# Layer 0's graph sum as a dense product over weights of node pairs, on one Trainium2 core

## The reference, cut to what matters

```python
edge_index = jnp.stack([src, dst])          # row = src, col = dst
def _L0_gnn_ref(x, edge_row, edge_col, edge_vals, w, b):
    deg = jax.ops.segment_sum(edge_vals, edge_row, num_segments=n)
    dinv = jnp.where(deg > 0, deg ** (-0.5), 0.0)
    norm_vals = edge_vals * dinv[edge_row] * dinv[edge_col]
    h = x @ w
    msg = norm_vals[:, None] * h[edge_col]
    agg = jax.ops.segment_sum(msg, edge_row, num_segments=n)
    return jax.nn.relu(agg + b)
x = x + _L0_gnn_ref(_layernorm(x, axis=-1), src, dst, edge_weight, L0_gnn_w, L0_gnn_b)
```

## Time and profile before

| what | value |
|---|---|
| median of 3 runs | 8010.51 us (8003.66 to 8014.09) |
| the profiled execution | 7996.99 us; span of its trace 7995.0 us |
| busy share of the span | PE 75%, PEld 54%, DVE 60%, ACT 37%, POOL 43% |
| mean granted clock of TensorE | 0.865 |
| DMA | 1231 MB, 154 GB/s over the span |

### The profile page before, as it was taken

One profiled execution on the slowest core, in us unless ns is written; L12 is line 12 of the kernel. 1 busy time (PEld: TensorE's weight loads), 2 busy tenths in 40 slices (PEclk: granted clock), 3 DMA queues, 4 the chain that ended last, 5 costly groups with the idle time before them and its releaser, 6 DMA issues. The chain is left out here.

```text
span 7995.0 us, 122318 instructions
## 1 busy us (share of the span) xinstructions
PE 5968.8 (75%) x30884; PEld 4285.4 (54%) x30885; DVE 4801.9 (60%) x10565; ACT 2966.1 (37%) x7906; POOL 3435.1 (43%) x2953
## 2 busy tenths in 40 slices
PE   7377566666663668788887696788887599587898
PEld 5155444444442435555565384566665488366666
DVE  7588533333333455788887625899998511687333
ACT  0033344444442224455554231454544333233333
POOL 1100188888884013777775041777775022000000
PEclk9855688888886779899998798999998799798999
DMA  3055699999997028777776143777776233321000
GB/s 157 31 176 177 170 190 191 189 188 186 189 191 188 4 69 318 219 230 230 231 230 162 44 135 105 231 234 239 238 236 168 101 111 103 121 99 39 8 12 20
DMA packets 671115, 1231.15 MB, mean 154 GB/s; under 512 B 93515, under 2 KB 477309, under 8 KB 658692
## 3 DMA queue, kind: packets, MB, share of 16 engines
q0 software_dynamic: 276016, 679.29, 33.9%
q1 hardware_dynamic: 388148, 540.62, 21.6%
q10 hardware_dynamic: 6560, 6.55, 0.3%
HBM read 902.62 MB, written 323.50 MB: 153 GB/s over the span
## 5 line engine op out<-in xcount | busy, mean ns | idle before, releaser
L2262 POOL DMA_INDIRECT rows<-l_kv,index_staged x1708 | 1721.4, 1008 | 706.6 <-issue 499.4
L1289 POOL DMA_INDIRECT gcn_sums<-out,target x806 | 1308.2, 1623 | 283.8 <-issue 156.8
L2375 PE MATMUL sum<-messages,hot 128*128 128x260 f32 (+1 forms) x3416 | 953.2, 408 | 53.5 <-issue 24.5
L2351 PE MATMUL q<-queries,spread 128*128 x5136 | 712.3, 285 | 129.0 <-DVE rows L2512 82.3
L2321 ACT ACTIVATE messages<-rows,messages 128x64 f32<-128x64 f32 (+1 forms) x3392 | 774.4, 323 | 0.0
L1309 PE MATMUL g<-same,hot 128*128 128x128 f32 x1612 | 319.0, 374 | 522.2 <-DVEq L1367 481.0
L2375 PEld LDWEIGHTS sum<-messages,hot 128*128 128x128 f32 x3416 | 606.4, 195 | 156.6 <-issue 74.0
L2512 DVE TENSOR_TENSOR rows<-q,rows 128x512 f32<-128x512 f32 x854 | 572.3, 683 | 142.2 <-DMA rows<-l_kv,index_staged 141.2
L2351 PEld LDWEIGHTS q<-queries,spread 128*128 128x128 bf16 x5136 | 483.3, 101 | 322.1 <-issue 218.2
L1309 PEld LDWEIGHTS g<-same,hot 128*128 128x128 f32 x1612 | 290.5, 277 | 619.4 <-issue 567.9
L1360 DVE TENSOR_SCALAR before<-before 128x13 f32<-128x13 f32 x62 | 11.3, 182 | 891.2 <-DMA gcn_sums<-out,target 890.6
(11 more groups left out here) (543 smaller groups left out, 11802.1 us busy)
## 6 DMA issues: line engine op xcount, KB each, us to landing
window<-gcn_rows SPq DMA_DIRECT2D x806, 128.0 KB
edge_counts<-count_stage SPq DMA_DIRECT2D x21, 3800.0 KB
rel<-slot_rel SPq DMA_DIRECT2D x218, 256.0 KB
src_row<-in_src_row SPq DMA_DIRECT2D x62, 832.0 KB
counts<-edge_counts SPq DMA_DIRECT2D x8, 4800.0 KB
first_part<-in_L_ffn_first SPq DMA_DIRECT2D x32, 1030.0 KB
rows<-l_kv,index_staged POOLq DMA_INDIRECT x1708
edge_attr<-in_attr SPq DMA_DIRECT2D x124, 208.0 KB
```

Of the source, the lines that this page charges most:

```text
L1289: pool.indirect_dma_start(out=copies[m], out_offset=bass.IndirectOffsetOnAxis(ap=target[:, u, j:j + 1], axis=0), in_=out[:, u, j, :], in_o ...
L2262: pool.indirect_dma_start(out=rows[:, u * 2 + n, j, :], out_offset=None, in_=table, in_offset=bass.IndirectOffsetOnAxis(ap=staged[:, u, n ...
L2351: ins = pe.matmul(q_ps[g % QUERY_BANKS][:, r, :], spread[:, t[1] * 2 + n, g * RUN % U + r, :], qs[:, bass.ds(tile, 1), m, :], start=m == 0 ...
L2375: ins = pe.matmul(sum_ps[g % 2][:, 0:W], hot[:, n, j, :], messages[:, n, j, :, :].rearrange("p h d -> p (h d)"), start=r == 0, stop=r == R ...
```

## The change

The sum of layer 0 is computed as a dense product: the weights of all edges between two nodes are added into a matrix of node pairs, and 625 float32 products (25 tiles of sources by 25 steps of 125 destinations) multiply it with the table's rows.

- The windows now take five nodes per group, so a key is one of 5 x 25 = 125 pairs; there are 97 windows in place of 108 and blocks of three windows (33, in place of 22 of five). Each window has two accumulations, each in four single-buffered PSUM banks: the counts as before (bf16) and the weights. For the weights VectorE multiplies the key one-hots with the edges' weights into float32 (`key_w`), ScalarE widens the lane one-hots to float32 (`lane_f`), and TensorE makes 15 more float32 products of 128 columns. ScalarE evicts both, and SyncE stores both for each block: counts as [128 partitions, 25, 5 x slots], weights as [125 partitions, slots, 128], with up to 46 slots in a block.
- `edge_units` also makes the weights of each unit: seven transpositions, seven ScalarE copies and 28 more products.
- `dense_sum` replaces `scatter_sum`. Its 75 steps (three groups of 10, 10 and 5 source tiles, 25 steps each) are loaded through a ring of six buffers by five DMAs of 25 partitions each; the table's rows lie in SBUF by step. The products stand between those of the edge perceptron, ten to a batch. At a group's end VectorE scales, adds bias and `x`.
- `clear_rows`, the seven copies, `CopySums`, relative positions and the count of loops fall away.

```diff
+        self.gcn_rows = nc.dram_tensor("gcn_rows", [NPAD, D], F32, kind="Internal").ap()
...
-NODES_EACH = 4
-COUNT_COLS = NODES_EACH * TILES
+NODES_EACH = 5
+PAIR_ROWS = NODES_EACH * TILES
...
-BLOCK_WINDOWS = 5
+BLOCK_WINDOWS = 3
...
+                pe.wait_ge(weight_in, 16)
+                for r, c, m in spans:
+                    real = min(m, CHUNKS - c)
+                    pe.transpose(key_ps[r // 4][0:real, r % 4 * P:(r % 4 + 1) * P], by_lane[:, c:c + real], k.ident[:, :]
+                                 ).then_inc(turned, 1)
+                pe.wait_ge(weight_rows, R)
...
+                for q, at, n in parts:
+                    pe.wait_ge(keyed, q + 1)
+                    for r, c, m in spans:
+                        ins = pe.matmul(key_ps[q][:, 0:n], weight[0:m, r, :], chosen[0:m, r, at:at + n],
+                                        start=r == 0, stop=r == R - 1)
+                ins.then_inc(weighed, 1)
...
+    k.pair_weights = nc.dram_tensor("pair_weights", [C, GROUP_SLOTS, P], F32, kind="Internal").ap()
...
+        count_stage = ph.sb("count_stage", [P, 2, TILES, BLOCK_SLOTS * E])
+        weight_stage = ph.sb("weight_stage", [P, 2, BLOCK_SLOTS * P])
+        count_ps, weight_ps = (ph.ps(n, [P, WINDOW_BANKS, 512]) for n in ("count_window", "weight_window"))
...
+                    dve.wait_ge(keys_hot, w + 1)
+                    shape = [P, U, C]
+                    dve.tensor_tensor(key_w[:, w % 2, :, :], hot_key[:, w % 2, :, :],
+                                      unit_w[:, w * U:(w + 1) * U].unsqueeze(2).to_broadcast(shape), ALU.mult
+                                      ).then_inc(keys_weighed, 1)
...
+                    begin(count_ps, P, C)
+                    if w:
+                        at = nc.snap(regs[U], min_val=0, max_val=(BLOCK_SLOTS - 1) * E)
+                        pe.matmul(counts[:, 0:C], k.ident[:, :], count_stage[:, last, :, bass.ds(at, E)].rearrange("p s e -> p e s"),
+                                  start=False, stop=False)
+                    pe.wait_ge(lanes_hot, w + 1)
+                    pe.wait_ge(keys_hot, w + 1)
                     for j in range(U):
                         at = nc.snap(regs[j], min_val=0, max_val=U * SLOT_COLS)
+                        pe.matmul(counts[:, bass.ds(at, C)], hot_lane[:, u, j, :], hot_key[:, u, j, :], start=False, stop=False)
+                    end(count_ps, P).then_inc(count_full, 1)
                     if w:
+                        pe.wait_ge(weight_kept, w)
+                    begin(weight_ps, C, P)
+                    if w:
+                        at = nc.snap(regs[U + 1], min_val=0, max_val=(BLOCK_SLOTS - 1) * P)
+                        pe.matmul(weights[0:C, 0:P], k.ident[0:C, 0:C], weight_stage[0:C, last, bass.ds(at, P)],
+                                  start=False, stop=False)
+                    pe.wait_ge(lanes_wide, w + 1)
+                    pe.wait_ge(keys_weighed, w + 1)
+                    for j in range(U):
+                        at = nc.snap(regs[j], min_val=0, max_val=U * SLOT_COLS)
+                        pe.matmul(weights[0:C, bass.ds(at, P)], key_w[:, u, j, :], lane_f[:, u, j, :], start=False, stop=False)
+                    end(weight_ps, C).then_inc(weight_full, 1)
...
+                def widen(w):
+                    act.wait_ge(lanes_hot, w + 1)
+                    act.activation(lane_f[:, w % 2, :, :], hot_lane[:, w % 2, :, :], ACT.Copy).then_inc(lanes_wide, 1)
...
+                            act.wait_ge(counts_stored, 16 * (b - 1))
+                            act.wait_ge(weights_stored, 16 * (b - 1))
...
+                    act.activation(weight_stage[0:C, b % 2, bass.ds(at, W * P)],
+                                   weight_ps[0:C, :, :].rearrange("p b c -> p (b c)"), ACT.Copy).then_inc(weight_kept, 1)
...
+                    sp.wait_ge(weight_kept, last)
+                    if b:
+                        sp.wait_ge(weights_stored, 16 * b)
+                    at = nc.snap(regs[1], min_val=0, max_val=GROUP_SLOTS - slots)
+                    sp.dma_start(k.pair_weights[:, bass.ds(at, slots), :],
+                                 weight_stage[0:C, b % 2, 0:slots * P].rearrange("p (g c) -> p g c", c=P)
+                                 ).then_inc(weights_stored, 16)
+                sp.wait_ge(counts_stored, 16 * BLOCKS)
+                sp.wait_ge(weights_stored, 16 * BLOCKS)
...
-def clear_rows(eng, tables, zeros, cleared):
...
+SUM_BANKS = 5
+SUM_TILES = 2 * SUM_BANKS
+KEYS = PAIR_ROWS // NODES_EACH
+STEP_NODES = KEYS * NODES_EACH
+STEPS_EACH = NODES // STEP_NODES
+SUM_STEPS = [(t, min(SUM_TILES, TILES - t), n) for t in range(0, TILES, SUM_TILES) for n in range(STEPS_EACH)]
+PRODUCTS = [(s, j) for s, (t, width, n) in enumerate(SUM_STEPS) for j in range(width)]
+PER_BATCH = len(PRODUCTS) // BATCHES
+SHARES = (1, 3, 5, 7, PER_BATCH)
...
+def dense_sum(k, table):
+
+    nc, a = k.nc, k.a
+    RING, S, E = 6, STEP_NODES, NODES_EACH
+    assert S * STEPS_EACH == NODES and S <= P
+    last_of = [PRODUCTS.index((s, width - 1)) // PER_BATCH for s, (t, width, n) in enumerate(SUM_STEPS)]
     with k.phase() as ph:
+        h = ph.sb("h_by_step", [P, STEPS_EACH, D])
+        pairs = ph.sb("pairs", [P, RING, SUM_TILES, P])
+        bias = ph.sb("gcn_bias", [P, D])
+        total = ph.sb("total", [P, 2, 2, D])
...
+        sum_ps = [ph.ps(f"sum{n}", [P, 2, D]) for n in range(SUM_BANKS)]
+        table_in, bias_in, pairs_in = ph.sem("table_in"), ph.sem("bias_in"), [ph.sem(f"pairs_in{n}") for n in range(RING)]
+        used, summed, emptied, scaled = (ph.sem(n) for n in ("used", "summed", "emptied", "scaled"))
+        weights = k.pair_weights.rearrange("(n t) g c -> n t g c", n=E)
+        rows = table[0:NODES, :].rearrange("(s g n) d -> n g s d", n=E, g=KEYS)
+        banks = [(t, b, min(2, width - 2 * b)) for t, width, n in SUM_STEPS if n == 0 for b in range(-(-width // 2))]
...
+                def load(s):
+                    t, width, n = SUM_STEPS[s]
+                    if s >= RING:
+                        sp.wait_ge(used, s - RING + 1)
+                    for e in range(E):
+                        sp.dma_start(pairs[e * KEYS:(e + 1) * KEYS, s % RING, 0:width, :],
+                                     weights[e, t:t + width, n * KEYS:(n + 1) * KEYS, :].rearrange("t g c -> g t c")
+                                     ).then_inc(pairs_in[s % RING], 16)
+                for e in range(E):
+                    sp.dma_start(h[e * KEYS:(e + 1) * KEYS, :, :], rows[e]).then_inc(table_in, 16)
+                for s in range(2):
+                    load(s)
                 mlp.load_weights(sp)
+                for b in range(BATCHES):
+                    if b >= 2:
+                        mlp.store(sp, b - 2, b % 2)
+                    mlp.load(sp, b, b % 2)
+                    if b == 0:
+                        sp.dma_start(bias[:, :], a["L0_gnn_b"].to_broadcast([P, D])).then_inc(bias_in, 16)
+                    for s in range(2, len(SUM_STEPS)):
+                        if b == (last_of[s - RING] + 1 if s >= RING else 0):
+                            load(s)
                 for u in range(2):
                     mlp.store(sp, BATCHES - 2 + u, u)
                     sp.wait_ge(mlp.stored[u], 64 * (BATCHES // 2))
...
+                for b in range(BATCHES):
+                    for col in range(2):
+                        for kk in range(KK):
+                            mlp.activate(act, b, col, kk)
+                    mlp.keep(act, b, b % 2)
...
+                pe.wait_ge(table_in, 16 * E)
+                def multiply(first, last):
+                    for s, j in PRODUCTS[first:last]:
+                        t, width, n = SUM_STEPS[s]
+                        if j == 0:
+                            pe.wait_ge(pairs_in[s % RING], (s // RING + 1) * (16 * E))
+                        if n == 0 and t and j % 2 == 0:
+                            pe.wait_ge(emptied, (t - SUM_TILES + j) // 2 + 1)
+                        ins = pe.matmul(sum_ps[j // 2][:, j % 2, :], pairs[0:S, s % RING, j, :], h[0:S, n, :],
+                                        start=n == 0 and j % 2 == 0,
+                                        stop=n == STEPS_EACH - 1 and (j % 2 == 1 or j == width - 1))
+                        if j == width - 1:
+                            ins.then_inc(used, 1)
+                        elif n == STEPS_EACH - 1 and j % 2:
+                            ins.then_inc(summed, 1)
+                for b in range(BATCHES):
+                    at = b * PER_BATCH
+                    multiply(at, at + SHARES[0])
+                    if b == 0:
+                        pe.wait_ge(mlp.w_in, 16 * (4 + JOBS))
+                    for q in range(4):
+                        mlp.hidden(pe, b, b % 2, q // 2, q % 2)
+                        multiply(at + SHARES[q], at + SHARES[q + 1])
+                    mlp.result(pe, b)
```

(55 more changed lines are left out.)

416 lines of the change are left out of this document (108 added, 308 removed).

## The result

The changed kernel takes 7890.0 us (median; 7882.8 to 7892.0) against 8012.3 for the kernel before, a ratio of 0.985 (0.983 to 0.986): 122 us faster, where 288 were forecast.

The account below looks back on a forecast made before the run. The prediction took layer 0's sum to be bound by a ring through scatters, about 25.8 us a batch. Terms -822, +601, -77 and +10 gave -288 us: 7997 to 7709, 7722 on the runs' median; range 7480 to 7970.

Parts of the forecast that it names:

- The sum: Sum of layer 0: batches of 11.3 us, loads hidden, 780 us in place of 1602, -822 us.
- The start: Start of the sum of layer 0: batch 0 runs from 45 to 57 us, batch 1 starts at 77.
- Routing: Routing of the feed-forward layer: without waiting for and adding seven copies, 125 us becomes 48, -77 us.
- smaller edits: Unit tables' last products, clearing the weight stage, one more barrier and degrees: together +10 us.
- The stores: Windows' stage: weights' stores on five engines set the pace at 32 us a block; 1075 us for 474, +601 us.
- TensorE's window: Windows' stage: TensorE takes 9 to 10.5 us a window, three of them below the stores' 32 us a block.
- rival 1: Windows' stage: stores spread over all engines, TensorE paces the windows; -470 us, kernel 7540; chance 0.2.
- The lower clock: Windows' stage: TensorE stays at 1.2 GHz, 12.8 us a window; the claim of rival 2, chance 0.17.
- rival 2: Windows' stage: TensorE stays at 1.2 GHz, 12.8 us a window, 1262 us; -101 us, kernel 7910; chance 0.17.
- Rival 3: Windows' stage: weights leave in 512-byte pieces, blocks of 42 to 65 us; kernel about 8350; chance 0.11.

Follow-up runs that it names:

- rows20: The changed kernel with rows of window places padded from 17 to 20 words, TensorE still loading 17 registers: 7698 us, ratio 0.961.
- both: The changed kernel with window-place rows padded to 20 words and weights stored from 128 partitions in place of 125: 7381 us, ratio 0.921.

## Why the prediction was wrong

- **The sum.** Right: 747 us for 780. A batch runs in 10.9 us (11.3 forecast) at a clock of 0.95 over the phase, and after the first product nothing waits for pairs, as the loads are hidden. The start is as told: the first product stands 36 us into the phase and batch 0's perceptron 46 (batch 0 was forecast from 45), and batch 1 begins at 76.5 (77) after a wait of 16.4 us for its attributes. Of the 33 us by which the sum beat 780, the 0.4 us of 61 batches are some 25.
- **Routing and smaller edits.** Routing right: -79 us (-77). The smaller edits were mis-sized: the phases ahead of the windows came out 18 us shorter, where the small edits together, some of them inside the windows' phase, were taken at +10.
- **The stores.** The mechanism and its size were right: five engines, 23 KB rows, a block of 32 us, 33.5 measured in `rows20`, where it was the last wait. But it wasn't what ended last in the changed kernel.
- **TensorE's window: the step that failed.** "I take 9 to 10.5" summed products alone, and three of these were held against the 32 us of the stores. The products took that, 871 us / 97 = 9.0. What it left out is the load of the window's registers, which the change lengthens from 16 words to 17 and so moves off multiples of 16 bytes. In the trace of before it took 1.1 us in the middle, and TensorE stood 0.25 us for it ahead of the L564 of the earlier trace rows and 91 us ahead of all of them; the sum passed over it. From the first to the last counts' issue of the changed kernel, 1258 us for 96 windows, TensorE was busy 8.8 us a window and stood idle 4.3, nearly all of it at this load: 13.1 in all, 39.3 us a block for 32. 7.3 us in each of 33 blocks are 241 us, what the phase missed (842 for 601).
- **The rivals.** Sixteen engines by themselves give 7797 us, not rival 1's 7540, for the same missing term. The lower clock held only in part (0.70 granted over the phase), and a 128-column product took 0.33 us of busy time in the mean (480.8 us for 97 x 15), not the 0.46 that was rival 2's sign. So it is chance that 7890 lies near rival 2's 7910. Its 12.8 us a window is also more than the terms listed for it, which add up to 11.9 to 12.4. Rival 3's pieces of 512 bytes, 5750 a block, weren't there: the changed kernel moved 7537 packets in all from 990 to 1080 us, more than two blocks.
- **The number.** 7890 lies inside the stated 7480 to 7970, and even inside the 7610 to 7940 for blocks of up to 36 us, though the blocks took 39.3. That is luck: the sum, the routing and the smaller edits came out 63 us better than forecast and hid part of the 241.

## What to carry to other kernels

An engine's register loads stand in its stream like any instruction: list them by source line, and look at what a change does to the place of each row, not only to the number of words. Pad such rows to a multiple of 16 bytes, and store from a number of partitions that sixteen divides (128 for 125 here). Two waits that cover each other must be taken away together: alone they gave 192 and 93 us here, together 509. Of the 224 us beyond their sum, about two thirds are TensorE's busy time in the windows' phase, which went from 871 to 726 us only with both edits (887 and 868 with either alone), at a granted clock of 0.88 for 0.70; the rest is idle time.

## What the runs showed of the hardware

- A register load of 17 words from SBUF took TensorE 1.36 us from a row on a multiple of 16 bytes and 4.03 us from any other, and both about three times as long (4.3 and 12 to 13 us) in the changed kernel while a store of 3200 rows of 920 bytes moved (1.6 to 4.3 us for the aligned ones of `both`). For 16 words it was 1.10 and 3.80 us. Whether the number of rows or the rate makes the second factor wasn't tried.
- A register load of six words beside such a store took ScalarE 2.5 us from a row on a multiple of 16 bytes and 4.9 to 5.0 from one 8 bytes past it.
- A store of 125 rows of 23552 bytes took 23.1 us in the middle at a DMA share of 0.28, one of 128 such rows 8.6.
- TensorE's granted clock over the windows' phase, for the same instructions, rose from 0.70 to 0.88 when its idle time there fell from 469 to 104 us.
